# Moving the second half's routing arithmetic behind the expert product on VectorE

## The chip, the cores and the metric

The kernel runs on one core of a Trainium2 chip. The metric is the device time of the kernel in microseconds (us), as the median of several executions. TensorE does the matmuls, VectorE and ScalarE the element-wise work between them, GpSimd (POOL) issues the indirect gathers and scatters, and SyncE (SP) issues the plain transfers.

## What is computed

A block of a transformer in three parts on 4096 tokens of width 128: half an expert layer, attention with 16 heads, and half an expert layer again, each behind a layer norm and added to its input. The change lies in the expert layer, which runs twice:

```
x = x + 0.5 * ffn(layernorm(x), ...)
x = x + attention(layernorm(x), ...)
x = x + 0.5 * ffn(layernorm(x), ...)

def ffn(x, router_w, gate_w, up_w, down_w):        # E = 8 experts, F = 512, top 2
    router_logits = x @ router_w.T
    top_vals, top_idx = jax.lax.top_k(router_logits, 2)
    routing_weights = jax.nn.softmax(top_vals, axis=-1)
    combine = jnp.sum(jax.nn.one_hot(top_idx, E) * routing_weights[..., None], axis=1)
    for e in range(E):
        g = x @ gate_w[e].T
        u = x @ up_w[e].T
        y = jax.nn.silu(g) * u @ down_w[e].T
        out = out + combine[:, e:e + 1] * y
```

## The kernel before

The tokens lie in 32 tiles of 128. Each expert layer (function `ffn`, lines 562 to 1236) first normalises them, writes the rows to memory, computes the router's logits, and sorts the (token, expert) pairs into 71 blocks of 128 rows, each block for one expert. The sorting ("routing") is made for the first 16 tiles before the loop. For the other 16 tiles ("routing 1") it is spread over the first steps of the loop, while blocks of the first half are being worked on.

The loop over blocks is written out by hand for each engine, from j = -1 to 73, and `step j` means the j-th pass in each engine's own order:

- POOL gathers the rows of block j + 4 once TensorE has transposed block j (L897), and scatters the finished rows of block j - 3 (L906).
- TensorE, in step j: transposes the product of block j - 2 (`turn_hidden`, L947), then the gathered rows of block j + 1 (`turn_rows`, L929), multiplies the transposed product of block j - 3 by the down weights (`project_down`, L957), and projects block j by gate and up weights (`project`: L938, L939 and L940, for gate and then for up). The transpose of rows waits for `xlo_ready` of the block before it, and so does `project`. In step 3 it runs two counting matmuls (L468 and L469) between the two transposes, in steps 12 to 15 eight matmuls each (L480), which also wait for the routing work they need (`both_ready`, `spot_ready`) and for `xlo_ready`.
- ScalarE, in step j: copies the transposed product of block j - 2 (L1008), the rounded high part of block j + 1 (L1019) and the result of block j - 3 (L1025) out of PSUM, and makes the silu of block j's gate (L1029).
- VectorE, in step j: computes the low part of block j + 1, which is the transposed rows less their high part (L1070, raises `xlo_ready`), then the piece of routing 1 that belongs to step j (`route_later`), in the first layer from step 47 on also a piece of preparing the attention's first tiles (`prepare_first`), and then the product of silu and up projection of block j (L1086, raises `hid_ready`; it waits for the silu and for the up matmuls of the same step).

`route_later` (L1089 to L1125) has a piece for steps 0 to 13 except 2, and for steps 15 to 20. Step 0 and step 1 find the best and the second best expert (`best_of`, L312), step 1 also writes `both` for the counting matmuls; step 3 sums (`totals`), step 4 makes sizes (`later_sizes`, L379), step 5 slots (L394), step 6 places, step 7 digits, steps 8 and 9 compare block numbers (L437, L448), steps 10 to 13 compare spots (L461), step 15 makes the list of sources, 16 of targets, 17 to 19 of owners (L531, L542 to L545, L553), 20 the weights. Most of their operations are chained: each waits for a semaphore that the one before it raises.

The engines take their instructions in the order written. What orders them against each other are semaphores alone.

Of the kernel before, what the change touches and what calls it, by code (L numbers as in the profile page):

```python
# [24 lines left out]
def wait(eng, sem, value):  # L25

    if isinstance(value, int) and value <= 0:
        return
    eng.wait_ge(sem, value)
# [532 lines left out]
def ffn(nc, name, X, xn_dram, ys_dram, gate_t, up_t, down_t, router_t, ident,  # L562
# [9 lines left out]
    with ExitStack() as ctx:  # L572
# [48 lines left out]
        with ExitStack() as early:  # L621
# [6 lines left out]
            with nc.Block() as block:  # L628
                @block.sync
                def _(sp):  # L630
                    sp.dma_start(router[:, :], router_t).then_inc(w_in, 16)
                    for n in range(PIECES):
                        sp.dma_start(piece(n)[1].bitcast(F32), (gate_t, up_t)[n // E][:, n % E, :]
                                     ).then_inc(w_part[n // E], 16)
                    for g in range(GROUPS):
                        if g < LEAD_GROUPS:
                            sp.wait_ge(xn_ready, g + 1)
                        else:
                            sp.wait_ge(xn_ready_pool, g - LEAD_GROUPS + 1)
                        sp.dma_start(xn_dram[4 * g * P:4 * (g + 1) * P, :].rearrange("(n p) d -> p n d", p=P),  # L640
                                     xn[:, 4 * g:4 * g + 4, :]).then_inc(xn_out, 16)
                    sp.dma_start(down[:, :, :, :], down_t).then_inc(down_in, 16)
                    sp.wait_ge(xn_out, 16 * GROUPS)
# [223 lines left out]
        def has(j, d):  # L867

            return 0 <= j + d < BLOCKS
# [5 lines left out]
        with nc.Block() as block:  # L875
# [182 lines left out]
            @block.vector  # L1058
            def _(dve):
                def step(dve, j, r):  # L1060
                    k = r % 2
                    if has(j, 1):
                        dve.wait_ge(xhi_ready, j + 2)
                        if j == COUNT_AT:
                            dve.wait_ge(routing.psum, Routing.COUNTED[1])
                            routing.link(dve.tensor_copy(routing.counts[:, :, :].rearrange("p a c -> p (a c)"),
                                                         later_counts))
                        if j == TAKE_AT:
                            routing.take_found(dve, 1, later_found)
                        dve.tensor_tensor(xt[1 - k][:, 1, :], x_bank[:, 0:P], xt[1 - k][:, 0, :].bitcast(F32),  # L1070
                                          ALU.subtract).then_inc(xlo_ready, 1)
                        if projection is not None and j in TURNED:
                            t = TURNED[j]
                            dve.wait_ge(first_hi, t + 1)
                            dve.tensor_tensor(first_XT[:, 1, t * P:(t + 1) * P], x_bank[:, P:2 * P],
                                              first_XT[:, 0, t * P:(t + 1) * P].bitcast(F32),
                                              ALU.subtract).then_inc(first_lo, 1)

                    route_later(j)
                    if projection is not None:  # L1080
                        prepare_first(j - SCATTERED - 3)
                    if has(j, 0):
                        dve.wait_ge(silu_ready, j + 1)
                        dve.wait_ge(gu_psum, 2 * j + 2)
                        wait(dve, hidT_psum, j - 1)
                        dve.tensor_tensor(hid[k][:, :], up_bank[k][:, :], silu[k][:, :],  # L1086
                                          ALU.mult).then_inc(hid_ready, 1)

                def route_later(j):  # L1089

                    if j == 0:
                        dve.wait_ge(logits_ready, 1)
                        routing.best_of(dve, 1, 0, routing.logits[:, :, :])
                    if j == 1:
                        routing.best_of(dve, 1, 1, routing.logits[:, :, :])
                        routing.both_of(dve, 1)
                        routing.gaps(dve, 1)
                    if j == COUNT_AT:
                        routing.totals(dve, 1, routing.counts[:, 1, :])
                    if j == 4:  # L1100
                        routing.later_sizes(dve)
                    if j == 5:
                        routing.slots(dve, 1, routing.counts[:, 0, :])
                    if j == 6:
                        routing.places(dve, 1)
                    if j == 7:
                        routing.digits(dve, 1)
                    if j in (8, 9):
                        routing.blocked(dve, 1, j - 8)
                        routing.numbered(dve, 1, j - 8)  # L1110
                    if 10 <= j < 14:
                        routing.spots(dve, 1, j - 10)
                    if j == TAKE_AT:
                        routing.join_found(dve)
                        routing.sources(dve, 1)
                    if j == TAKE_AT + 1:
                        routing.targets(dve, 1)
                    if j == TAKE_AT + 2:
                        routing.passed(dve, 1)
                    if j == TAKE_AT + 3:  # L1120
                        routing.owner_of(dve, 1)
                    if j == TAKE_AT + 4:
                        routing.pack(dve, 1)
                    if j == TAKE_AT + 5:
                        routing.shares(dve, 0, exp_ready)  # L1125

                def prepare_first(m):

                    some = slice(0, 4)
                    if 0 <= m < 4:  # L1130
                        k = m // 2
                        dve.wait_ge(first_in, 32)
                        if k:
                            dve.wait_ge(first_added, 2 * (m - 2) + 2)
                        for t in (2 * (m % 2), 2 * (m % 2) + 1):
                            dve.scalar_tensor_tensor(out=X[:, t, :], in0=first_got[:, k, t, :],
                                                     scalar=wts[:, 2 + k, t:t + 1], in1=X[:, t, :],
                                                     op0=ALU.mult, op1=ALU.add).then_inc(first_added, 1)
                    if m in (4, 5):
                        dve.wait_ge(first_added, 8)  # L1140
                        for t in (2 * (m - 4), 2 * (m - 4) + 1):
                            dve.bn_stats(stats[:, t, :], X[:, t, :]).then_inc(first_stats, 1)
                    if m == 6:
                        dve.wait_ge(first_stats, 4)
                        variances(link, dve, some, stats, mean, rstd, tmpa, tmpb)
                    if m == 7:
                        guess(link, dve, some, mean, rstd, tmpa)
                    if m in (8, 9, 10):
                        refine(link, dve, some, rstd, tmpa, tmpb)
                    if m == 11:  # L1150
                        dve.tensor_tensor(first_shift[:, :], mean[:, some], rstd[:, some], ALU.mult
                                          ).then_inc(first_shifted, 1)

                def trailing(m):
                    part = slice(m * 512, (m + 1) * 512)
                    dve.wait_ge(all_hi, m + 1)
                    dve.tensor_tensor(at_lo[:, part], w_all[:, part], at_hi[:, part].bitcast(F32),
                                      ALU.subtract).then_inc(all_lo, 1)

                link = routing.link = moments.link  # L1160
                link.eng = dve
                routing.passed(dve, 0)
                routing.owner_of(dve, 0)
                routing.pack(dve, 0)
                routing.targets(dve, 0)
                for j in range(-1, BLOCKS + 3):
                    step(dve, j, j % AHEAD)
                    if projection is not None and j - 1 in SPLIT:
                        trailing(SPLIT[j - 1])
                if projection is None:  # L1170
                    routing.shares(dve, 1, exp_ready)
# [672 lines left out]
```

## Time and profile before

| | us |
|---|---|
| median of three runs | 1329.45 |
| lowest and highest run | 1326.75, 1330.23 |
| the profiled execution: all of it | 1330.23 |
| the profiled execution: its span, first to last instruction | 1328.2 |
| first layer's loop over blocks, about | 57 to 264 |
| second layer's loop over blocks, about | 1086 to 1292 |

The mean granted clock of TensorE in the profiled execution is 0.962 of full speed. In the rows below, times are from the start of the span. PE is the matmuls and PEld the weight loads of TensorE, DVE is VectorE, ACT is ScalarE. L with a number is a line of the kernel. An operation is written as output<-inputs by the names of the tiles: f_xt holds the high and low part of a block's rows, f_hid the product, f_xb the gathered rows, f_b a PSUM bank.

### The profile page before, as it was taken

The page shows a single profiled execution, that of the slowest core. Times are in us where ns is not written, and L with a number is a line of the kernel's source. Part 1 is how long each engine was busy: PE and PEld are TensorE (multiplying, and loading weights), DVE is VectorE, ACT ScalarE, POOL GpSimd, SP SyncE. Part 2 cuts the span into 40 slices and gives each one's busy share as a digit, 9 for nine tenths or more (in the row PEclk, how much of TensorE's full clock was granted, in tenths as well). Part 3 has the DMA queues.
Part 4 walks back from the last instruction along what each step waited for, and adds up shares of the span by engine and source line. Part 5 has one row for each costly group of instructions (what it writes and reads, how often), then busy time and mean ns, then how long its engine had stood idle before and what let it go on. Part 6 is the DMA issues. An engine that isn't in the chain of part 4 may idle for free. (4 is left out here: it accounts for less than half of the span.)

```text
span 1328.2 us, 27053 instructions
## 1 busy us (share of the span) xinstructions
PE 1226.3 (92%) x8148; PEld 904.7 (68%) x8148; DVE 937.3 (71%) x2015; ACT 788.0 (59%) x2237; POOL 846.1 (64%) x911
## 2 busy tenths in 40 slices
PE   7699999969999999999999999999998879999990
PEld 5488888846666666666666666666665658888880
DVE  5775345358888888888888888888887587533325
ACT  5565665636666666666666666665565466555552
POOL 4367776548677667677676676676665237766652
PEclk7799999979999999999999999999999789999995
DMA  9311121122221222222122222112220611111117
GB/s 305 121 41 49 47 64 47 39 68 49 64 49 41 56 48 65 49 49 60 39 47 65 49 49 65 40 42 48 49 49 17 216 55 42 48 47 49 47 37 194
DMA packets 86474, 86.45 MB, mean 65 GB/s; under 512 B 10496, under 2 KB 77056, under 8 KB 85824
## 3 DMA queue, kind: packets, MB, share of 16 engines
q1 hardware_dynamic: 73024, 63.99, 18.0%
q0 software_dynamic: 9088, 18.63, 5.0%
q10 hardware_dynamic: 4224, 2.10, 0.5%
q8 instruction: 73, 1.20, 0.4%
q14 instruction: 65, 0.53, 0.1%
HBM read 35.53 MB, written 15.60 MB: 38 GB/s over the span
## 5 line engine op out<-in xcount | busy, mean ns | idle before, releaser
L1489 POOL TENSOR_SCALAR at_prob<-at_prob,at_rec 128x128 f32<-128x128 f32 (+3 forms) x256 | 315.7, 1238 | 215.6 <-DVE at_rec L1659 214.7
L1756 ACT ACTIVATE at_prob<-at_s,at_nb 128x128 f32<-128x128 f32 (+3 forms) x512 | 265.2, 526 | 49.0 <-DVE at_nb L1651 44.3
L1765 ACT ACTIVATE at_probT<-at_pt 128x128 f32<-128x128 f32 (+3 forms) x256 | 104.9, 436 | 230.6 <-PE at_pt L1584 230.6
L1651 DVE TENSOR_REDUCE at_nb<-at_s 128x2 f32<-128x256 f32 (+3 forms) x256 | 208.7, 816 | 6.9 <-PE at_s L1570 6.9
L906 POOL DMA_INDIRECT ys_dram<-y,f_target x142 | 141.8, 999 | 92.1 <-issue 65.5
L1086 DVE TENSOR_TENSOR f_hid<-f_b,f_silu 128x512 f32<-128x512 f32 x142 | 98.5, 694 | 143.5 <-PE f_b L940 120.9
L897 POOL DMA_INDIRECT f_xb<-xn_dram,f_source x142 | 143.9, 1013 | 84.8 <-issue 41.4
L1584 PE MATMUL at_pt<-ident,at_prob 128*128 128x128 f32 x1280 | 184.1, 275 | 1.8 <-DVE at_prob L1662 1.2
L1565 PE MATMUL at_s<-at_KT,at_QT 64*128 64x128 f32 (+3 forms) x1024 | 174.6, 459 | 5.4 <-DMA at_KT<-at_R 4.1
L1645 DVE TENSOR_TENSOR at_turned<-at_pj,rope 128x1024 f32<-128x1024 f32 x122 | 148.9, 1220 | 40.1 <-PE at_pj L1531 40.1
L1483 POOL TENSOR_TENSOR at_R<-at_turned 128x512 f32<-128x512 f32 x128 | 159.5, 1265 | 12.6 <-DVE at_turned L1645 12.6
L1596 PE MATMUL at_o<-at_probT,at_V 128*64 128x512 f32 (+3 forms) x1024 | 152.0, 437 | 16.2 <-DVE at_probT L1669 16.2
L1584 PEld LDWEIGHTS at_pt<-ident,at_prob 128*128 128x128 f32 x1280 | 141.0, 141 | 23.9 <-issue 12.9
L957 PE MATMUL f_b<-f_down,f_hidT 128*128 x1136 | 150.4, 275 | 1.7 <-ACT y L1025 1.2
L1596 PEld LDWEIGHTS at_o<-at_probT,at_V 128*64 128x64 f32 x1024 | 80.8, 136 | 98.8 <-issue 76.5
L957 PEld LDWEIGHTS f_b<-f_down,f_hidT 128*128 128x128 f32 x1136 | 138.2, 192 | 2.5 <-issue 2.5
L1662 DVE TENSOR_SCALAR at_prob<-at_prob,at_rec 128x128 f32<-128x128 f32 (+3 forms) x256 | 122.8, 480 | 9.1
L1669 DVE COPY at_probT<-at_pt 128x128 f32<-128x128 f32 (+3 forms) x256 | 119.2, 486 | 9.9 <-PE at_pt L1584 2.2
L1008 ACT ACTIVATE f_hidT<-f_b 128x512 f32<-128x512 f32 x142 | 84.7, 597 | 69.2 <-PE f_b L947 69.1
L1029 ACT ACTIVATE f_silu<-f_b 128x512 f32<-128x512 f32 x142 | 85.0, 599 | 58.6 <-PE f_b L940 58.5
L1565 PEld LDWEIGHTS at_s<-at_KT,at_QT 64*128 64x128 f32 x1024 | 78.0, 187 | 53.5 <-issue 24.7
L1756 ACT ACTIVATION_READ_ACCUMULATOR at_prob<-at_s,at_nb 128x1 f32 x512 | 104.0, 203 | 0.0
(287 smaller groups left out, 2156.6 us busy)
## 6 DMA issues: line engine op xcount, KB each, us to landing
at_QT<-at_R SPq DMA_DIRECT2D x128, 128.0 KB, 2.4
at_KT<-at_R SPq DMA_DIRECT2D x128, 128.0 KB, 2.4
f_gate<-gate_t SPq DMA_DIRECT2D x16, 256.0 KB, 4.9
f_up<-up_t SPq DMA_DIRECT2D x16, 256.0 KB, 6.6
xn_dram<-f_xn SPq DMA_DIRECT2D x16, 256.0 KB, 4.6
f_down<-down_t SPq DMA_DIRECT2D x2, 2048.0 KB, 8.0
f_got<-ys_dram SPq DMA_DIRECT2D x16, 256.0 KB, 4.9
at_got<-ys_dram SPq DMA_DIRECT2D x14, 256.0 KB, 3.2
```

The costliest lines, as they stand in the source:

```text
L897: pool.indirect_dma_start(out=xb[j % AHEAD][:, :], out_offset=None, in_=xn_dram, in_offset=bass.IndirectOffsetOnAxis(ap=routing.source[:, ...
L906: pool.indirect_dma_start(out=ys_dram, out_offset=bass.IndirectOffsetOnAxis(ap=routing.target[:, j:j + 1], axis=0), in_=y[k][:, :], in_off ...
L957: one = pe.matmul(y_bank[:, 0:P], hidT[k][:, c, :], down[:, bass.ds(e, 1), c, :].rearrange("p a d -> p (a d)"), start=(c == 0), stop=(c == ...
L1483: pool.tensor_tensor(R[:, :, cols], turned[0][:, :, cols], turned[1][:, :, cols], ALU.add).then_inc(r_ready, 1)
L1489: pool.tensor_scalar(w, w, rec[:, q, 1:2], None, ALU.mult).then_inc(probB_ready, 1)
L1565: pe.matmul(s_bank[q % 2][:, h, 0:n], q_tile[rows, q * P:n], k_tile[rows, 0:n], start=True, stop=False)
L1584: one = pe.transpose(pt_bank[h][:, at:at + P], prob[q][:, h, b * P:(b + 1) * P], ident[:, :])
L1596: one = pe.matmul(o_bank[64 * h:64 * h + 64, b * P:SEQ], V[(i // 4) % 2][:, b, 128 * j + 64 * h:128 * j + 64 * h + 64], probT[h][:, b, b * ...
L1645: dve.tensor_tensor(turned[half][:, :, :], src, rope[:, half, :, :], ALU.mult).then_inc(rope_ready, 1)
L1651: dve.tensor_reduce(nb[:, q, :], s_bank[q % 2][:, :, 0:(q + 1) * P], axis=AX, op=ALU.max, negate=True).then_inc(nb_ready, 1)
L1662: dve.tensor_scalar(w, w, rec[:, q, 0:1], None, ALU.mult).then_inc(probA_ready, 1)
L1756: act.activation(prob[q][:, h, :], s_bank[q % 2][:, h, 0:n], ACT.Exp, bias=nb[:, q, h:h + 1], scale=1.0, accum_out=sums[:, q, h:h + 1]).th ...
```

## The change

In VectorE's program the call of `route_later(j)` is taken out of `step`, where it stood between the low part of block j + 1 and the product of block j, and put behind `step` in the loop, so that it follows the product of block j and precedes, in the first layer, `trailing` (which splits weights of the attention, steps 31 to 41) and the low part of block j + 2. It holds for both layers.

```
                                               ALU.subtract).then_inc(first_lo, 1)
 
-                    route_later(j)
                     if projection is not None:
                         prepare_first(j - SCATTERED - 3)
                     if has(j, 0):
...
                 for j in range(-1, BLOCKS + 3):
                     step(dve, j, j % AHEAD)
+                    route_later(j)
                     if projection is not None and j - 1 in SPLIT:
                         trailing(SPLIT[j - 1])
```

The routing functions, the semaphores and the programs of the other engines stay as they are.

## Rows read from the trace of the kernel before

**Rows 1.** The page, busy time of each engine.

```profile
PE 1226.3 (92%) x8148; PEld 904.7 (68%) x8148; DVE 937.3 (71%) x2015; ACT 788.0 (59%) x2237; POOL 846.1 (64%) x911
```

**Rows 2.** TensorE's waits, 57 to 265 us: total us, times, longest.

```profile
PE f_b L929 <- DMA f_xb<-xn_dram,f_source: 10.0, 2, 8.5
```

**Rows 3.** Timeline, step 21: start us, duration us, instruction [idle before it <-releaser].

```profile
120.53 0.47 PE L938 MATMUL f_b<-f_gate,f_xt 128*128 x1
...
121.77 0.60 PEld L947 LDWEIGHTS f_b<-ident,f_hid 128*128 128x128 f32 x4
...
122.26 0.69 DVE L1086 TENSOR_TENSOR f_hid<-f_b,f_silu 128x512 f32<-128x512 f32 x1 [1.37 <-PE f_b L940]
122.34 0.14 PEld L929 LDWEIGHTS f_b<-ident,f_xb 128*128 128x128 f32 x1
...
123.36 0.47 PE L938 MATMUL f_b<-f_gate,f_xt 128*128 x1
```

**Rows 4.** Timeline, steps 4 and 5 of the first layer.

```profile
70.83 0.48 PE L938 MATMUL f_b<-f_gate,f_xt 128*128 x1
...
71.12 0.16 DVE L383 TENSOR_TENSOR f_size<-f_row,f_lead_count 128x8 f32<-128x8 f32 x1
...
73.14 0.17 DVE L392 TENSOR_TENSOR f_step<-f_later,f_begun 128x8 f32<-128x8 f32 x1
73.34 0.69 DVE L1086 TENSOR_TENSOR f_hid<-f_b,f_silu 128x512 f32<-128x512 f32 x1
...
75.76 0.29 DVE L411 TENSOR_TENSOR f_row<-f_row,f_base 128x128 f32<-128x128 f32 x1
```

**Rows 5.** Timeline, steps 0 to 3 of the second layer.

```profile
1088.61 0.28 DVE L319 TENSOR_REDUCE f_best<-f_logits 128x16 f32<-128x128 f32 x1
...
1090.22 0.29 DVE L327 SCALAR_TENSOR_TENSOR f_rest<-f_chosen,f_logits 128x128 f32<-128x128 f32 x1
...
1090.86 0.69 DVE L1086 TENSOR_TENSOR f_hid<-f_b,f_silu 128x512 f32<-128x512 f32 x1 [0.36 <-PE f_b L940]
...
1091.47 0.28 DVE L1070 TENSOR_TENSOR f_xt<-f_b,f_xt 128x128 fp32r<-128x128 f32 x1
...
1091.67 0.28 DVE L319 TENSOR_REDUCE f_best<-f_rest 128x16 f32<-128x128 f32 x1
...
1093.69 0.83 DVE L1086 TENSOR_TENSOR f_hid<-f_b,f_silu 128x512 f32<-128x512 f32 x1
...
1094.58 0.42 PEld L947 LDWEIGHTS f_b<-ident,f_hid 128*128 128x128 f32 x4 [0.46 <-DVE f_hid L1086]
...
1094.96 0.10 PEld L468 LDWEIGHTS f_b<-f_both,const_less 128*128 128x128 bf16 x1
```

**Rows 6.** Timeline, step 18 of the first layer.

```profile
112.29 1.44 DVE L542 TENSOR_REDUCE f_ownerf<-f_past 128x52 f32<-128x1248 f32 x1
...
114.35 0.19 DVE L545 CAST f_ownerf<-f_owner_i 128x52 f32<-128x52 int32 x1
```

**Rows 7.** Timeline, step 8 of the first layer, the second of two such operations.

```profile
83.44 0.93 DVE L448 TENSOR_TENSOR f_named<-f_in_block,const_numbersb 128x736 bf16<-128x736 bf16 x1
```

**Rows 8.** Timeline, steps 0 and 3 of the first layer.

```profile
62.65 0.69 DVE L1086 TENSOR_TENSOR f_hid<-f_b,f_silu 128x512 f32<-128x512 f32 x1 [0.30 <-PE f_b L940]
...
66.85 0.10 PEld L468 LDWEIGHTS f_b<-f_both,const_less 128*128 128x128 bf16 x1
```

**Rows 9.** Windows: stretch, its length, busy us of each engine, PEclk, DMA share, GB/s.

```profile
57.00:64.00 7.00, 5.06 (x13) 3.79 (x14) 3.54 (x12) 2.71 (x5) 2.83 (x3) 0.50 0.65 226
296.00:299.00 3.00, 3.00 (x17) 2.58 (x14) 2.49 (x7) 2.30 (x10) 1.77 (x2) 0.52 0.00 0
1012.00:1024.00 12.00, 10.68 (x84) 6.95 (x80) 8.62 (x20) 6.63 (x22) 6.51 (x6) 1.00 0.00 1
```

**Rows 10.** Timeline and, last, the page's DMA issues (KB, median us to landing).

```profile
83.54 1.68 POOL L906 DMA_INDIRECT ys_dram<-y,f_target  x1 [0.58 <-issue]
...
f_xb<-xn_dram,f_source POOLq DMA_INDIRECT x142, 2.6
```

More of the change, by code:

```diff
@@ L1077, in step @@
                                               ALU.subtract).then_inc(first_lo, 1)
-                    route_later(j)
                     if projection is not None:
@@ L1167, in _ @@
                     step(dve, j, j % AHEAD)
+                    route_later(j)
                     if projection is not None and j - 1 in SPLIT:
```

## The prediction

> **What bounds the kernel now.** I read the page's busy shares first [rows 1]: TensorE is busy 92% of the span, VectorE 71%. Then the stretch that the change touches, the loops over 71 blocks of the two expert layers (57 to 264 us and 1086 to 1292 us). There the list of TensorE's waits [rows 2] begins with the wait for the first gathered rows (10.0 us in two waits), which lies ahead of the loop's steady part; nothing of weight follows it. So TensorE sets the pace, and everything that VectorE does in the loop is hidden. The timeline of a step without routing work [rows 3] shows how: the first gate matmul of block 21 starts at 120.53 and that of block 22 at 123.36. I call the first P(j), and take 2.84 us for its period (this one is 2.83; others are 2.84 or 2.85, and four steps with the matmuls of L480 are longer by TensorE's own work). In P's terms the low part of x for block j+1 (L1070) starts a moment after P, once ScalarE has made the high part, the product hid of block j (L1086) at P+1.73, and TensorE's weight load for the transpose of the next rows (L929) at P+1.81.
>
> So VectorE's cycle is hid(j-1), low part of j+1, [routing j], hid(j). What must be ready when decides the case. Hid(j) is asked for by TensorE in step j+2 only, by the transposes at L947, whose first load comes 121.77 - 120.53 = 1.24 after that step's predecessor began, so at P+2.84+1.24 = P+4.08 for a product that could be done at P+2.42. It has 1.66 us to spare, and routing before it eats only that. The low part of block j+2 (VectorE's step j+1) is asked for by TensorE in step j+2 ahead of its row transpose (L929 waits for xlo_ready of j+2), with loads at P+2.84+1.81 = P+4.65. Behind that transpose stand project_down and the six matmuls of project, which the engine takes in order: what holds L929 holds all.
>
> **The change, part by part.** Nothing is added or removed: the same instructions run, and routing work of step j moves from ahead of hid(j) to behind it, which is ahead of the low part of j+2. No DMA is issued by the moved code, no queue of SP is passed.
>
> *What it gives.* Hid(j) starts at P+1.73 instead of up to P+2.51 (73.34 - 70.83, [rows 4]). TensorE waits for a late hid in one place: at 1094.58 [rows 5], 0.46 us of idle, in the second layer. All other late products are inside their 1.66 us. Where VectorE is not the limit, this is worth nothing.
>
> *What it costs in a plain step.* Hid starts at P+1.73; the instruction after a hid starts 0.61 after it (1090.86 to 1091.47, [rows 5]), so routing starts at P+2.34. With R for the length of the routing piece and 0.03 for the gap behind it (73.14 + 0.17 to 73.34), the low part starts at P+2.37+R, takes 0.29, and TensorE sees it 0.06 later (hid ends at 1093.69 + 0.83 = 1094.52, load at 1094.58). Required: P+2.37+R+0.35 <= P+4.65, so R up to 1.93 is free.
> - Step 4 (later_sizes, ten small chained operations): 71.12 to 73.31, R = 2.19, over by 0.26 [rows 4].
> - Step 5 (slots): hid(4) starts at 73.34, and routing follows by 0.61 and 0.20 ([rows 5], below) at 74.15, to 76.05, R = 1.90, free [rows 4]; it also begins late, since hid(5) waits for the delayed low part: that starts at P(4)+4.56, hid(5) 0.20 later at P(4)+4.76, and P(5) = P(4)+2.84, so hid(5) is at P(5)+1.92 and the next low part 0.19 late; but TensorE itself has become 0.26 later by step 4, which covers it. Nothing more.
> - Step 18 (owner_of): 112.29 to 114.54, R = 2.25, over by 0.32 [rows 6].
> - The longest of the others are steps 8 and 9, two operations of 0.93 each, 1.86 [rows 7]: free.
> So 0.58 us per layer from steps 4 and 18.
>
> *What it costs at the opening.* Here blocks 0 and 1 come with nothing behind them, and two long pieces follow each other: route(0) takes 1.90 (1088.61 to 1090.22 + 0.29, [rows 5]) and route(1) more. Second layer, by the rows: hid(0) waits for TensorE and stays at 1090.86. Route(0) then starts at 1091.47, ends at 1093.37; the low part of block 2 starts at 1093.40 (before: 1091.47); hid(1) 0.20 behind its start (as 1091.47 to 1091.67) at 1093.60 (before: 1093.69, so nothing is gained there); route(1) at 1094.21. In the kernel before, route(1) began at 1091.67 and the hid behind it ended at 1094.52, that is 2.85 later; less hid's 0.69 (the record of this hid, 0.83, begins early; a plain one is 0.69) and with the low part's 0.28 in its place, the low part of block 3 ends 2.44 after route(1) starts, at 1096.65. The counting matmuls (L468, step 3) wait for both_ready of route(1) and for that low part: their load moves from 1094.96 to 1096.71. Cost 1.75 us. First layer, same walk from hid(0) at 62.65 [rows 8]: +0.61 +1.90 +0.03 +0.20 +0.61 +2.44 +0.06 = 68.50, against 66.85 before: 1.65 us. Behind this point nothing catches up, since the steps after it are TensorE's own 2.84 us.
>
> *Sum.* 1.65 + 1.75 + 2 x 0.58 = 4.56 us; I take 4.55. All of it is on the path: the first loop's end releases the attention, the second loop's end the last combination, and no fixed time stands between. Bounds: below, if the first blocks run longer at the low clock (the granted level in 57 to 64 us is 0.50, half of full speed, [rows 9]), TensorE needs the low parts later; with that in both layers the opening costs perhaps 1 us each, sum 3.2. Above, each of the six holds could cost 0.1 more for semaphores, and steps 8 and 9 (R = 1.86, just free) could tip over by 0.1 each in both layers, with as much again for their followers: 4.56 + 0.6 + 0.5 = 5.7.
>
> *The POOL queue.* Gathers and scatters wait for TensorE and ScalarE, not for the moved code. But VectorE's wide bf16 operations lie beside them: the scatter at 83.54 took 1.68 us [rows 10] against 1.0 for most. The change moves these operations from P+0.3 to P+2.3 (above), from beside the scatter to beside the gather. The gather comes behind the row transpose at P+1.8, for rows four blocks on, say at P(j)+2.6 against their need at P(j+3)+1.8 = P(j)+10.3, 7.7 us later, and lands in 2.6 us [rows 10], so 0.7 us more is covered with 4 us in hand; without that cover the ten or so collisions of a layer would cost up to 7 us. Cost taken: nothing. The Trainium skill (SBUF — State Buffer, "SBUF: two separate sides" and "Who interferes with whom") says that a tensor_tensor takes only the read interface of the port pair that VectorE and GpSimd share, and infers that it doesn't hold up descriptor generation; the row at 83.54 is longer beside just such an operation, so this case's trace does not agree. By the skill's inference the collisions cost nothing wherever they lie, by the row they cost 0.7 us each, hidden: the sum is the same.
>
> **The rivals.**
> - *The hold is filled or not felt (no change, not slower).* If the low part is not what TensorE needs first, or if project_down, which fills most of the 1.0 us from L929 to the next P (122.34 to 123.36, [rows 3]), can run in front of a held transpose, every hold under some 0.9 us is free: steps 4 and 18 vanish, and of the opening some 0.8 per layer stays or less, against which the freed hid(1) gives back 0.2. Time 1329 to 1331. It decides if TensorE can start anything behind L929. Against it: at 1094.58 the array stood idle for 0.46 us before L947 while the count, the row transpose and project_down behind it had their inputs. The Trainium skill (TensorE: Matmul & The Clock Gate, part 2, step by step) says that only weight loads are pulled ahead and matmuls stay in program order; by it this rival falls, and the row at 1094.58 agrees. 17 in 100.
> - *The clock falls in the holds.* The holds of 1 us each come just after the level rises. At half speed [rows 9] a step that TensorE fills grows from 2.84 towards 5.7, and as VectorE is the limit in these steps, 1 to 2 us of that would show in each layer: 2 to 4 us more, 1336 to 1338. Against it: in the attention TensorE idles 1.3 of 12 us at a level of 1.00 [rows 9]. 10 in 100.
> - *Faster, by the levels of the attention's start.* The first steps of the attention run at changing levels (0.52 in 296 to 299 us, with TensorE busy throughout, [rows 9]). Shifted by 2 us, such a stretch may fall away, worth at most half of those 3 us, and the runs of before spread over 3.5 us as it is. With the smallest holds, or with none, and scatter in its favour, that gives 1325 to 1327 against 1329.45. 8 in 100, of both this and plain scatter.
> - *Rows arrive late.* The POOL queue falls behind by more than its 4 us: 1336 and up. Needs collisions at every step. 4 in 100.
>
> **How the numbers follow.** The profiled execution took 1330.23 us in all, 1328.2 of them span; with 4.55 it would be 1334.8. It is the slowest of three, 0.8 above the median 1329.45, so against the median I forecast 1334.0, which is slower by 0.34%. A difference under 0.3% (4.0 us) can hardly be told from none here, so my own forecast stands at that border. The forecast has 61 in 100, its own range 1332.6 to 1335.2 (3.2 and 5.7 on the median); of it I count 36 as slower and 25 as within. Clock and late rows add 14 to slower, the filled hold 15 to within and 2 to faster, the last rival 5 to faster and 3 to within. Slower 0.50, same 0.43, faster 0.07. The range reaches from the filled hold's upper part to the clock's: 1329.5 to 1337.5.
>
> **What the profile would show.** In the timeline of the second layer: hid(0) unmoved relative to the first row transpose, six operations of route(0) behind it, the low part of block 2 some 1.9 us later, TensorE idle ahead of the load at L929 for about 1 us and ahead of L468 for another, the counting load 5.85 after hid(0) starts (before 4.10). Then holds of 0.2 to 0.3 us at L929 of steps 6 and 20, and steps of 2.84 us everywhere else. In the list of TensorE's waits a new entry, f_b L929 or L468 held by VectorE's L1070, of some 4 us in all. The prediction is wrong if that entry is missing, if the clock row shows a new low stretch in the loops, or if a wait for f_xb appears behind block 1.

## The result and the profile after

The changed kernel takes 1335.81 us in the median of 19 runs, against 1329.91 for the kernel before, also 19 runs. The medians differ by 5.90 us. The ratio is 1.0052, which is 6.9 us, with a 95% interval of 1.0038 to 1.0066: slower by 5.1 to 8.8 us, and beyond the 0.3% that the prediction named. The forecast was 1334.0 and slower by 0.34%, at the border. The measured median lies 0.6 us above the forecast's own range (1332.6 to 1335.2) and inside the wider one (1329.5 to 1337.5); the sum of the losses was too small.

The profiled execution after took 1333.55 us with a span of 1331.5. Its page still shows TensorE as the engine that sets the pace, with the busy shares of [rows 1]:

```profile
PE 1228.6 (92%) x8148; PEld 905.1 (68%) x8148; DVE 935.3 (70%) x2015; ACT 788.1 (59%) x2237; POOL 847.6 (64%) x911
```

The list of TensorE's waits for the second loop (1086 to 1296 us; total, times, longest) answers to [rows 2]. Two entries are new, and both name the low part (L1070); the first line below is the old wait for gathered rows:

```profile
PE f_b L929 <- DMA f_xb<-xn_dram,f_source: 5.7, 2, 4.9
PE f_b L929 <- DVE f_xt L1070: 0.7, 1, 0.7
PE f_b L468 <- DVE f_xt L1070: 0.5, 1, 0.5
```

The list counts only the time in which the matmuls' records leave the array idle, 1.2 us here; in the first loop only L468 has such an entry, 0.4 us. The prediction had expected some 4 us in this list in all. What the loop lost is larger and is seen between the starts of the first gate matmul of each block, the P(j) of the prediction. Between P(0) and P(70) the first loop took 203.16 us (before 200.39), the second 203.10 (before 199.91): +2.77 and +3.19, together 5.96 us. Where it was lost, and what the prediction had, per layer in us:

| place | predicted | first loop | second loop |
|---|---|---|---|
| P(0) to P(3), pieces 0 and 1 | 1.65, 1.75 | 1.77 | 1.91 |
| P(6), piece 4 | 0.26 | 0.28 | 0.28 |
| P(10), P(11), pieces 8 and 9 | 0 | 0.10 | 0.36 |
| P(20), piece 18 | 0.32 | 0.60 | 0.61 |
| sum, with 0.02 to 0.03 scattered | 4.56 in both | 2.77 | 3.19 |

All other steps are as long as before. The opening of the second layer in the timeline of after, to be read beside [rows 5]:

```profile
1091.21 0.69 DVE L1085 TENSOR_TENSOR f_hid<-f_b,f_silu 128x512 f32<-128x512 f32 x1 [2.10 <-PE f_b L940]
1091.82 0.28 DVE L319 TENSOR_REDUCE f_best<-f_logits 128x16 f32<-128x128 f32 x1
...
1093.76 0.29 DVE L1070 TENSOR_TENSOR f_xt<-f_b,f_xt 128x128 fp32r<-128x128 f32 x1
...
1093.97 0.68 DVE L1085 TENSOR_TENSOR f_hid<-f_b,f_silu 128x512 f32<-128x512 f32 x1
...
1094.16 0.14 PEld L929 LDWEIGHTS f_b<-ident,f_xb 128*128 128x128 f32 x1 [0.93 <-issue]
...
1096.58 0.42 DVE L1070 TENSOR_TENSOR f_xt<-f_b,f_xt 128x128 fp32r<-128x128 f32 x1
...
1097.06 0.10 PEld L468 LDWEIGHTS f_b<-f_both,const_less 128*128 128x128 bf16 x1 [0.69 <-DVE f_xt L1070]
```

VectorE now idles 2.10 us ahead of hid(0), in which piece 0 used to be done. The piece follows 0.61 behind, the low part of block 2 comes at 1093.76, which is 2.55 after hid(0) started (predicted 2.54), and TensorE's load at L929 waits 0.93 us for it. The counting load comes 5.85 after hid(0) started, which is the predicted number. (This hid is L1085 in the changed kernel, one line less than before.)

Of the 5.96 us the profiled execution shows 3.3 in its span. The stretch between the loops, P(70) to the next P(0), was 2.27 us shorter than in the profile before. The windows of the second layer's preparation, before and then after (length, busy us of each engine, granted clock):

```profile
1035.00:1087.00 52.00, 40.34 (x220) 30.09 (x220) 37.28 (x122) 30.26 (x62) 16.04 (x24) 0.81 0.50 165
```

```profile
1035.00:1088.00 53.00, 40.08 (x234) 30.04 (x230) 37.01 (x123) 30.72 (x62) 16.39 (x25) 0.84 0.49 162
```

TensorE's clock stood at the upper of its two levels, 2.4 GHz, for more of this stretch (mean granted clock 0.84 against 0.81). In the eight experiments' profiles from the same chip the stretch between the loops ran from 2.06 us shorter to 4.43 us longer than in the profile of before, whatever the edit. So it is scatter of single executions. The loops' 5.96 us lies inside the timed interval of 5.1 to 8.8, near the 5.90 of the medians and below the 6.9 of the ratio. How near is in part luck, since the opening of the kernel before scatters too: P(0) to P(3) is 8.41 and 8.34 us in its profile, and 8.31 to 9.11 in the seven experiments on this chip that leave the opening as it was. With pieces 0 and 1 behind hid (the changed kernel and open_behind below) it is 10.18 to 10.24.

### The profile page after: what moved, and what is told of

Its sections match the earlier page's. It is cut to its first block and busy times, and to the rows that moved or that the text cites. A ratio compares the mean times of both kernels' runs of the same rounds, so it can differ in the third digit from the quotient of the medians.

```text
span 1331.5 us, 27055 instructions
## 1 busy us (share of the span) xinstructions
PE 1228.6 (92%) x8148; PEld 905.1 (68%) x8148; DVE 935.3 (70%) x2015; ACT 788.1 (59%) x2237; POOL 847.6 (64%) x911
## 5 line engine op out<-in xcount | busy, mean ns | idle before, releaser
L1085 DVE TENSOR_TENSOR f_hid<-f_b,f_silu 128x512 f32<-128x512 f32 x142 | 98.1, 691 | 161.9 <-PE f_b L940 126.9
L897 POOL DMA_INDIRECT f_xb<-xn_dram,f_source x142 | 147.4, 1038 | 85.4 <-issue 39.5
L957 PE MATMUL f_b<-f_down,f_hidT 128*128 x1136 | 151.3, 276 | 1.8 <-ACT y L1025 1.3
L957 PEld LDWEIGHTS f_b<-f_down,f_hidT 128*128 128x128 f32 x1136 | 138.2, 192 | 3.7 <-issue 3.4
```

Source lines behind the costliest of these rows:

```text
L897: pool.indirect_dma_start(out=xb[j % AHEAD][:, :], out_offset=None, in_=xn_dram, in_offset=bass.IndirectOffsetOnAxis(ap=routing.source[:, ...
L957: one = pe.matmul(y_bank[:, 0:P], hidT[k][:, c, :], down[:, bass.ds(e, 1), c, :].rearrange("p a d -> p (a d)"), start=(c == 0), stop=(c == ...
```

## Experiments

**Which pieces cost.** Four kernels place some pieces of `route_later` ahead of hid and the others behind it. In `step` and in the loop, with the condition of each:

```
+                    if COND:
+                        route_later(j)
                     if projection is not None:
                         prepare_first(j - SCATTERED - 3)
...
                     step(dve, j, j % AHEAD)
-                    route_later(j)
+                    if not (COND):
+                        route_later(j)
```

*open_ahead*, COND `j in (0, 1)`. 

> Pieces 0 and 1 stand ahead of hid as before, all others behind it. Theory A (the loss is made where TensorE is held at L929 and L468, piece by piece): the opening's share goes, 1.77 + 1.91 us by the traces of before and after, and holds of 0.28 (piece 4) and 0.60 (piece 18) per layer stay, with 0.1 to 0.3 around pieces 8 to 11: about +2.0 us over before. Theory B (the loss comes from the changed order as a whole, by clock levels or the place of instructions in the program, not by pieces): about the +5.9 of the full change, or any value unrelated to the pieces.

*open_behind*, COND `j not in (0, 1)`. 

> Only pieces 0 and 1 stand behind hid. Theory A: the opening's share alone, +3.7 us over before, P(3) - P(0) 1.8 to 1.9 us longer in each layer, and every later step as long as before. Theory B: no relation to the pieces; near 0 or near +5.9.

*long_behind*, COND `j not in (4, 18)`. 

> Only pieces 4 and 18 (R = 2.19 and 2.25 us) stand behind hid. Theory A: 2 x (0.28 + 0.60) = +1.8 us over before, holds ahead of P(6) and P(20) alone. By my prediction's formula without any cost behind the hold: 2 x (0.26 + 0.32) = +1.2. Theory B: no relation.

*rest_behind*, COND `j in (0, 1, 4, 18)`. 

> Pieces 3, 5 to 13, 15 to 17, 19 and 20 stand behind hid, the others ahead. Theory A: R under 1.93 is free, so within 0.3 us of before (0.1 at step 11 and 0.35 at step 10 of the second layer, if what the trace of after shows there is not chance). Theory B: a part of +5.9 in proportion to the moved instructions, +3 or more.

Measured, in us over before: by the ratio of the timed runs with its interval (on 1330.12), and by P(0) to P(70) of both loops in the profiles of this and of before.

| kernel | timed | interval | by the loops | of it away from P(2), P(3) |
|---|---|---|---|---|
| open_ahead | +1.7 | -0.1 to +3.5 | +2.05 | 2.1 |
| open_behind | +2.8 | +0.9 to +4.7 | +3.66 | 0 |
| long_behind | -0.4 | -2.4 to +1.6 | +2.27 | 1.7 |
| rest_behind | +1.6 | -0.5 to +3.7 | +1.49 | 1.1 |

The last column leaves out P(2) and P(3), which also move by up to 0.6 us with the moment at which the clock rises, in kernels whose opening is that of before (the granted clock from 63.5 to 65 us is 0.83 in the kernel before and 0.50 in long_behind, whose P(2) comes 0.55 later). Theory A holds: in open_behind the two loops lose the 1.76 and 1.90 us of the full change ahead of P(3), and no later step differs by 0.05. In long_behind the losses stand at P(6), 0.29, and at P(20), 0.49; the timed runs don't confirm them, since their interval ends at 1.6, just below the 1.7 of the traces. The expectation for rest_behind (within 0.3) was wrong: with piece 4 out of the way, piece 5 (R = 1.90) costs 0.27 and 0.24 at P(7), and pieces 8 and 9 cost 0.11 and 0.14 at P(11), though the formula had 1.93 us free. That is a second sign, beside piece 18, that the limit lies lower. The other 0.31 us are at P(20), 0.16 and 0.15, and are no matter of the limit: piece 17 behind one product and piece 18 ahead of the next make hid(18) late (it ends at 116.84 in the first loop), and TensorE's load at L947 waits for it until 116.89.

**What a piece may take.** The kernel before gets two more operations on VectorE in every third step from 22 to 61, 14 places in each loop, either behind `step` or in `step` ahead of hid. Their results are not used.

```
+                def fill(count):
...
+                    link(dve.tensor_tensor(past, place, row_of(routing.ends[:, 0:ends], count, ends), ALU.is_ge))
...
                     step(dve, j, j % AHEAD)
+                    if j in range(22, 62, 3):
+                        fill(52)
+                        fill(23)      # 6 in fill18, 39 in fill26
```

*fill18_behind*. 

> The kernel before, with two more VectorE operations (R about 1.78 us together) behind hid in every third step from 22 to 61 of both layers, 28 places. Theory A with the limit of 1.93 us: nothing, 0 us, no hold. If the limit were lower (1.6, say), +5 us or more.

*fill22_behind*. 

> As the one before with R about 2.20 us. By the formula alone (2.20 - 1.93 = 0.27 per place): +7.6 us. With the 0.25 that piece 18 cost beyond its formula at each place: +14.6 us. If TensorE could run project_down in front of the held transpose: 0.

*fill26_behind*. 

> R about 2.60 us behind hid. By the formula alone 0.67 per place: +18.8 us; with 0.25 more at each place +25.8. The difference to R = 2.20 is 0.40 per place, +11.2, in both cases. If project_down filled the hold: 0.

*fill26_ahead*. 

> The same operations (R about 2.60 us) ahead of hid, in the old place. Theory A: hid ends at P+3.6, asked for at P+4.08, and the low part of the block after is 0.6 late with 1.3 us in hand: 0 us. If VectorE's time counted wherever it lies: as much as behind hid.

| kernel | timed over 1329.92 | interval | second loop | per place there |
|---|---|---|---|---|
| fill18_behind | +6.1 | +3.7 to +8.4 | +2.43 | 0.14 |
| fill22_behind | +17.0 | +14.6 to +19.3 | +7.83 | 0.56 |
| fill26_behind | +29.8 | +27.5 to +32.1 | +13.37 | 0.96 |
| fill26_ahead | +2.3 | +0.1 to +4.5 | +0.01 | 0 |

(The last column is the sum from P(24) to P(63), over 14. The first loop lost 0.13 more per place on average behind hid, nearly all of it at three places, P(33), P(39) and P(57), where the filler met `trailing` and `prepare_first`.) The expectation for fill18_behind was nothing, and was wrong. The recorded R of the second and third is 2.22 and 2.62. Each microsecond beyond the limit costs one: 0.40 more of R, 0.40 more per place. The line meets zero at R = 1.66, not at 1.93, and 1.78 already costs. The same 2.62 us ahead of hid cost nothing in the second loop. In the first they cost 1.0 us, of which 0.75 at P(57), where four operations of `prepare_first` stand ahead of the same product and TensorE waits for it, a late product beyond its 1.66 us in hand:

```profile
222.42 0.42 PEld L947 LDWEIGHTS f_b<-ident,f_hid 128*128 128x128 f32 x4 [0.77 <-DVE f_hid L1087]
```

The timeline of fill26_ahead in the second loop shows hid late, and TensorE's loads where they are in a plain step:

```profile
1163.50 2.62 DVE L1134 TENSOR_TENSOR f_past<-const_first_place,f_ends 128x1248 f32<-128x1248 f32 x2
1166.15 0.69 DVE L1087 TENSOR_TENSOR f_hid<-f_b,f_silu 128x512 f32<-128x512 f32 x1
```

```profile
1167.30 0.60 PEld L947 LDWEIGHTS f_b<-ident,f_hid 128*128 128x128 f32 x4
1167.87 0.14 PEld L929 LDWEIGHTS f_b<-ident,f_xb 128*128 128x128 f32 x1
```

The transposes of this hid begin at 1167.30, 0.46 us behind its end. So at 2.62 us it is the place of the work, not its amount, that costs.

**What a hold costs beyond the wait.** Step 20 of the first loop in the timeline of after:

```profile
116.39 1.44 DVE L542 TENSOR_REDUCE f_ownerf<-f_past 128x52 f32<-128x1248 f32 x1
...
118.43 0.19 DVE L545 CAST f_ownerf<-f_owner_i 128x52 f32<-128x52 int32 x1
...
118.66 0.29 DVE L1070 TENSOR_TENSOR f_xt<-f_b,f_xt 128x128 fp32r<-128x128 f32 x1
...
119.06 0.14 PEld L929 LDWEIGHTS f_b<-ident,f_xb 128*128 128x128 f32 x1 [0.34 <-issue]
...
119.42 0.97 PEld L957 LDWEIGHTS f_b<-f_down,f_hidT 128*128 128x128 f32 x8 [0.22 <-issue]
```

The low part starts at P(18) + 4.62 (114.04), as the formula says. The load at L929 follows its end by 0.11, not 0.06. And project_down's first load follows L929 by 0.36 us, where a plain step has 0.10 (the load at 122.34 in [rows 3]; L957's follows at 122.44). In fill22_behind the idle time ahead of L929 is 0.32 (once 0.33) in all 14 places of the second loop, but that second distance is 0.22 in two and 0.30 to 0.36 in the others, by the step's place in a group of four (steps 24 and 30):

```profile
1164.28 0.14 PEld L929 LDWEIGHTS f_b<-ident,f_xb 128*128 128x128 f32 x1 [0.32 <-issue]
1164.64 0.97 PEld L957 LDWEIGHTS f_b<-f_down,f_hidT 128*128 128x128 f32 x8 [0.22 <-issue]
...
1182.46 0.14 PEld L929 LDWEIGHTS f_b<-ident,f_xb 128*128 128x128 f32 x1 [0.32 <-issue]
1182.68 0.97 PEld L957 LDWEIGHTS f_b<-f_down,f_hidT 128*128 128x128 f32 x8
```

What repeats by four in TensorE's program is the way in which the number of the expert is worked out of the packed list (`all_seven // E ** d % E`). Hence this edit to fill22_behind:

```
+                always = pe.value_load(const.numbers_i[0:1, 0:1], min_val=0, max_val=E - 1)
                 for first in range(-1, BLOCKS + 3, 4):
...
-                    known = seven_owners(low)
+                    known = [always] * 7
```

*fill22_onereg*. 

> As fill22_behind, but every block takes the weights of expert 0 by one register that is loaded once ahead of the loop, instead of a number worked out of a packed list (this leaves out the choice of the expert). In front of project_down's first matmul TensorE's program then has one plain register operation in every step, where the other kernels have it in one step of four and a longer form in three. Theory S (what a hold costs beyond its formula is the work of TensorE's sequencer behind the held transpose, which is hidden while a backlog of matmuls stands in front of it): the extra falls where the long form stood, so that all 14 places of the second loop lose 0.46 us, as its steps 30, 42 and 54 did, +6.4 us instead of +7.83. Theory R (the extra is the array's own restart, or the semaphore's way): the places keep their 0.46 to 0.60, +7.8 us.

It ran, with the three below, on another chip, where the kernel before takes 1399.55 us in the median and steps are lengthened by another wait (last section), so that its total (a ratio of 0.9932, 0.9905 to 0.9958) can't be set against fill22_behind, and the 6.4 us were not to be read. (It is less than the kernel before takes on that chip, in spite of the added work; it leaves out the choice of the expert, and the load of the packed list with it. Why it gains so much was not followed up.) The distance can be, since it is measured behind a held load:

```profile
1225.02 0.14 PEld L929 LDWEIGHTS f_b<-ident,f_xb 128*128 128x128 f32 x1 [0.92 <-issue]
1225.14 0.97 PEld L957 LDWEIGHTS f_b<-f_down,f_hidT 128*128 128x128 f32 x8
```

It is 0.12 or 0.13 in 33 of the 34 places where L929 had been held (0.68 in the other), after holds of 0.31 to 2.54 us, against 0.21 to 0.44 in all 27 of fill22_behind. It isn't the chip: gaps_step2 (below) ran on the same one with numbers worked out as usual, and in the ten places where L929 was held there the distance is 0.21 to 1.38, never less. So Theory S holds, and more than it expected: not only the difference by four, nearly the whole extra was the sequencer's register work. Theory R is out, since the array restarts in the same way in both. That the total would fall by as much was not shown.

**Is it the order on TensorE?** `project_down` is written ahead of `turn_rows`, in the changed kernel and in the one before:

```
+                        if has(j, -3):
+                            project_down(j - 3, 1 - k, known[j - 3 - (low - 3)])
                         if has(j, 1):
...
                             turn_rows(j + 1, (j + 1) % AHEAD)
-                        if has(j, -3):
-                            project_down(j - 3, 1 - k, known[j - 3 - (low - 3)])
```

*down_first_after*. 

> The changed kernel with project_down(j - 3) written ahead of turn_rows(j + 1) on TensorE, so that 0.97 us of loads stand in front of the transpose that waits for the low part. If the holds are made at L929 because everything behind it waits: the holds of pieces 4 and 18 (0.28 and 0.60 per layer) go, those of the opening stay, since there is no project_down before step 3 and the counting matmuls stay ahead of it: about +3.7 us over before. If the holds are made elsewhere: +5.9 as for the full change. If the order on TensorE has a price of its own, the control shows it.

*down_first_before*. 

> The control: the kernel before with project_down ahead of turn_rows. Routing stands ahead of hid, where it has 1.66 us in hand; the high and low parts come about 0.6 us later in the step and hid of the long pieces later by as much, still inside. 0 us, steps of 2.84 us as before.

Against the kernel before on that chip they took +13.0 us (8.8 to 17.1) and +9.1 (5.9 to 12.2), so the order has a price there, which I had put at 0; where it arises I did not follow up. The difference of their medians is 3.4 us, near the 3.7 expected, but the two intervals overlap. In the profiles P(0) to P(3) is 10.17 in both loops with routing behind hid and 8.74 and 8.36 with routing ahead, +3.24 together. P(20), held by 0.60 in the changed kernel, is hardly late any more: P(19) to P(20) is 2.96 and 2.92, where a plain step has 2.84 and the changed kernel 3.44. In the first loop the late low part starts at 126.45, and TensorE runs the loads of project_down meanwhile:

```profile
126.45 0.29 DVE L1070 TENSOR_TENSOR f_xt<-f_b,f_xt 128x128 fp32r<-128x128 f32 x1
126.72 0.97 PEld L957 LDWEIGHTS f_b<-f_down,f_hidT 128*128 128x128 f32 x8
127.61 0.14 PEld L929 LDWEIGHTS f_b<-ident,f_xb 128*128 128x128 f32 x1
```

So the loads in front of the held transpose cover most of this hold, and such a late low part costs because everything stands behind L929. P(6) can't be read: P(5) to P(6) is 3.44 and 3.40, but 3.46 and 3.44 in the control too. There the step is some 0.6 us longer through another wait (project_down's load at L957 idles 0.57 us at 78.35 in down_first_after), and the low part waits for ScalarE's copy, not for piece 4.

**A version that might beat both.** The kernel before has one late product, hid(1) of the second layer. The last operation of piece 1 moves to the free step 2:

```
                         routing.both_of(dve, 1)
+                    if j == 2:
                         routing.gaps(dve, 1)
```

*gaps_step2*. 

> The kernel before with the last operation of piece 1 (gaps, needed only behind the loop) moved to step 2, which has no piece. Hid(1) is the only product that TensorE waits for; it should come some 0.2 us earlier, and P(3) - P(2) of the second layer be 0.2 shorter, of the first 0.1: -0.3 us, too little for the timed runs, to be read in the trace. If hid(1) isn't late because of piece 1: no change there.

Timed it is the same as before (1.0002, 0.9985 to 1.0020). Its timeline at 1126 us:

```profile
1126.21 0.71 DVE L333 TENSOR_TENSOR f_both<-f_chosen 128x128 bf16<-128x128 f32 x1
1126.56 0.89 DVE L1086 TENSOR_TENSOR f_hid<-f_b,f_silu 128x512 f32<-128x512 f32 x1
...
1127.50 0.42 PEld L947 LDWEIGHTS f_b<-ident,f_hid 128*128 128x128 f32 x4 [0.81 <-DVE f_hid L1086]
...
1127.64 0.17 DVE L338 TENSOR_TENSOR wts<-f_best 128x16 f32<-128x16 f32 x1
```

Hid(1) ends 2.84 us behind the start of route(1) (1124.61), where before it was 2.85. The operation that I moved had cost nothing: it lay in the shadow of `both_of` (L333), whose 0.71 us hid has to wait out in either order. The expectation was wrong. No version here beats the kernel before.

## Why the prediction was right, and what it mis-sized

- *TensorE sets the pace, and the changed order makes it wait for the low part ahead of L929 and L468.* Shown: by the new entries in its waits, by open_behind, by the fill kernels behind and ahead of hid, and by P(20) of down_first_after.
- *Late products had 1.66 us in hand, so nothing was gained by making them early.* Shown: 2.62 us ahead of hid are free in the second loop, and cost where `prepare_first` comes on top. One late product, hid(1) of the second layer, was outside its 1.66 us; gaps_step2 shows that moving the last operation of piece 1 doesn't make it earlier.
- *The opening, 1.65 and 1.75.* Measured 1.77 and 1.91. The chain on VectorE is right to 0.01 us (5.85 from hid(0) to the counting load). The rest, 0.12 and 0.16, came behind it: project_down's first load follows the count's 0.39 later (1097.06 to 1097.45), where before it was 0.22 (1094.96 to 1095.18).
- *A plain step's limit of R = 1.93.* This is the term that was mis-sized: the line through R = 2.22 and 2.62 meets zero at 1.66. The 0.27 us are the semaphore's way (0.11 instead of 0.06) and the 0.12 to 0.26 of sequencer work behind the held load. The formula asked when TensorE's load would start; what counts is whether its sequencer stays ahead of the array. (In the second loop of fill18_behind no hold at L929 is recorded at all, and yet project_down's load follows it by 0.14 to 0.29 us in the 14 places.) Piece 18 cost 0.60 for 0.32 by it, and pieces 8 and 9 a tenth for nothing.
- *Piece 4, 0.26*, measured 0.28, by two errors that cancel: the low part started at P(4) + 4.43 instead of 4.56, because one operation of the piece was shorter this time, and the extra behind the hold was its smallest, 0.12.
- *Clock, POOL queue, filled hold.* Behind its rise in the opening (a mean of 0.52 from 1088 to 1092 us) the clock stayed at its upper level, 1.00 from 1092 to 1292. No wait for f_xb appeared behind block 1, and nothing ran behind a held L929. The collisions on GpSimd were longer than the 1.68 us that the prediction read, and still hidden: beside piece 17's comparison (L531, 128x1248) a gather took 2.01 us:

```profile
113.83 2.01 POOL L897 DMA_INDIRECT f_xb<-xn_dram,f_source  x1 [0.30 <-issue]
```

- *The sum*: 4.56 predicted, 5.96 by the profiles, 5.90 by the medians, 6.9 by the ratio. The upper bound had been 5.7, and the 0.1 per hold that it allowed for semaphores was too little for what stood behind the holds. That the median still lies in the wider range is luck in this sense: its part above 1335.2 had been given to the falling clock and the late rows, and neither came.
- Not settled: the 0.36 us at P(10) of the second loop. Hid(8) started there at P + 2.10 with its inputs done at 1114.58:

```profile
1115.03 0.69 DVE L1085 TENSOR_TENSOR f_hid<-f_b,f_silu 128x512 f32<-128x512 f32 x1 [1.23 <-PE f_b L947]
```

In the two other profiles from this chip with piece 8 behind hid, open_ahead and rest_behind, hid(8) starts at P + 1.74 and P + 1.75, and this loss is absent.

## What to carry to other kernels

On an engine that is not the bottleneck, ask for each piece of filler work not how long it is but which result comes next behind it, and when that is asked for. Here 2.6 us of work was free ahead of a result with 1.66 us in hand, for which VectorE would have waited idle anyway (1.37 us in [rows 3]). It cost from 1.66 us on when it stood ahead of a result that the bottleneck's queue meets first. (The two 1.66 are different measures.) And a wait on the busiest engine costs more than the lateness: add what its sequencer had done in the shadow of the backlog.

## What the runs showed of the hardware

- Behind a held weight load (L929) the next load, whose address is worked out at run time, came 0.21 to 0.44 us later (fill22_behind, 27 places), with the address from one fixed register 0.12 or 0.13 (fill22_onereg, 33 of 34), and 0.10 in an unheld stream ([rows 3], to 122.44).
- Beside a VectorE comparison of 128x1248 f32 GpSimd's gather took 2.01 us, against 0.97 for most: once in each loop of the changed kernel (113.83 in the first) and 24 times in fill22_behind, whose filler is such an operation.
- Two chips differ by 5% on the same kernel, 1330.12 and 1399.55 us. In the loop of the slower (gaps_step2, which is the kernel before but for one small operation) ScalarE waits at L1025, from 1150 to 1290 us:

```profile
ACT y L1025 <- remote: 41.0, 18, 2.6
```

The kernel before has no such entry on the other chip. L1025 writes a buffer of y and waits for the scatter that last read it, so the scatters are the likely cause, but it isn't shown: the profiles from the slower chip have no landing times of gathers and scatters, and the packets of the queue that carries both took no longer there. In gaps_step2 (packets, MB, share of 16 engines' span; 5.0% in the kernel before):

```profile
q0 software_dynamic: 9088, 18.63, 4.7%
```

The cause of the difference between the chips stays open.
